# Bilinear hats of a deformable convolution: distances from ACT replaced by differences of clamped ramps

## The reference

```
def _bilinear_sample(x, py, px):
    y0 = jnp.floor(py); x0 = jnp.floor(px)
    for dy in (0.0, 1.0):
        for dx in (0.0, 1.0):
            yi = y0 + dy; xi = x0 + dx
            wy = 1.0 - jnp.abs(py - yi); wx = 1.0 - jnp.abs(px - xi)
            valid = (yi >= 0) & (yi < Hh) & (xi >= 0) & (xi < Ww)
            out = out + x[:, clip(yi), clip(xi)] * (wy * wx * valid)[None]
```

## Time and profile before

| | us |
|---|---|
| runs | 4312.64, 4316.48, 4319.70 |
| median | 4316.48 |
| span of the profiled execution | 4314.1 |
| PE, PEld busy | 3880.1 (90%), 2973.5 (69%) |
| DVE, ACT, POOL busy | 2952.5 (68%), 2786.4 (65%), 1140.5 (26%) |
| mean granted clock of PE | 0.94 of full speed |

### The profile page before, as it was taken

One profiled execution on the slowest core, in us unless ns is written; L12 is line 12 of the kernel. 1 busy time (PEld: TensorE's weight loads), 2 busy tenths in 40 slices (PEclk: granted clock), 3 DMA queues, 4 the chain that ended last, 5 costly groups with the idle time before them and its releaser, 6 DMA issues.

```text
span 4314.1 us, 221726 instructions
## 1 busy us (share of the span) xinstructions
PE 3880.1 (90%) x81908; PEld 2973.5 (69%) x81908; DVE 2952.5 (68%) x5858; ACT 2786.4 (65%) x6651; POOL 1140.5 (26%) x645
## 2 busy tenths in 40 slices
PE   4998799699789879979988997998799999799998
PEld 3776577477567657756765775776577777577776
DVE  5885687488567668847856884784577774577775
ACT  2885588388478658837865883885355554255554
POOL 0441243134033214403322431331111110111111
PEclk8999899799989989989998997999799999899999
DMA  4442544344244334424424443443766664666664
GB/s 125 127 127 66 143 125 110 89 126 127 75 132 126 90 106 127 125 76 131 126 71 127 127 114 92 126 125 109 179 154 152 150 150 127 147 154 152 152 150 110
DMA packets 244838, 533.50 MB, mean 124 GB/s; under 512 B 61200, under 2 KB 151824, under 8 KB 227216
## 3 DMA queue, kind: packets, MB, share of 16 engines
q1 hardware_dynamic: 194224, 498.67, 45.0%
q10 hardware_dynamic: 50240, 29.89, 2.4%
HBM read 471.87 MB, written 56.45 MB: 122 GB/s over the span
## 4 chain that ended last, share of the span: by engine, by line
PE 68%; SPq 18%; issue 7%; ACT 2%; DMA 2%; DVE 2%; POOLq 0%; ACTq 0%; DVEq 0%; POOL 0%; PEld 0%; PEldq 0%
PE P L544 26%; PE PS L562 24%; SPq L380 9%; PE P L515 8%; PE PS L575 8%; SPq L388 8%; SPq L370 1%; PE PS L515 1%; ACT H L848 1%; DMA X<-x_dram 1%; PE P L530 1%; DVE FOFF L1032 1%; DMA VT<-ht_store 0%; DVE A L917 0%; DVE ST L1036 0%
## 5 line engine op out<-in xcount | busy, mean ns | idle before, releaser
L917 DVE TENSOR_TENSOR A<-P,YC 121x384 f32<-121x384 f32 (+1 forms) x4608 | 2311.4, 550 | 850.1 <-ACT YC L768 684.5
L544 PE MATMUL P<-HL,SEL 32*121 32x384 f16 (+1 forms) x21504 | 1745.6, 304 | 131.6 <-issue 95.3
L768 ACT ACTIVATE YC<-P 121x384 f32<-121x384 f32 (+1 forms) x4608 | 1733.9, 444 | 98.7 <-PE P L544 65.8
L544 PEld LDWEIGHTS P<-HL,SEL 32*121 32x121 f16 (+1 forms) x21504 | 1126.9, 117 | 513.9 <-issue 228.6
L562 PE MATMUL PS<-A,VT 121*32 121x80 f32 (+1 forms) x40960 | 1342.7, 250 | 51.7 <-DMA VT<-ht_store 15.5
L562 PEld LDWEIGHTS PS<-A,VT 121*32 121x32 f32 (+1 forms) x40960 | 1093.0, 117 | 354.6 <-issue 200.4
L1103 POOL CAST HL<-DIST 128x1152 f16<-128x1152 f32 x320 | 366.3, 1145 | 3066.1 <-DVE DIST L922 3043.8
L745 ACT ACTIVATE SMP<-PS 128x480 f32<-128x480 f32 (+3 forms) x1152 | 593.9, 516 | 638.2 <-PE PS L562 632.9
L1105 POOL TENSOR_TENSOR HL<-DIST,HL 128x1152 f16<-128x1152 f32 x320 | 769.6, 2405 | 58.5 <-POOL HL L1103 58.5
L735 ACT ACTIVATE DIST<-HB,CONST 128x1152 f32<-128x1152 f32 x320 | 400.8, 1252 | 231.4 <-DMA HB<-off_store 128.8
L575 PE MATMUL PS<-SMP,CW 128*64 128x128 f32 x7424 | 476.0, 277 | 5.4 <-ACT SMP L745 5.4
(11 more groups left out here) (61 smaller groups left out, 703.4 us busy)
## 6 DMA issues: line engine op xcount, KB each, us to landing
HB<-off_store SPq DMA_DIRECT2D x2560, 72.0 KB
VT<-ht_store SPq DMA_DIRECT2D x256, 512.0 KB
VT<-ht_store SPq DMA_DIRECT2D x768, 132.0 KB
VT<-ht_store SPq DMA_DIRECT2D x256, 88.0 KB
off_store<-FOFF SPq DMA_DIRECT2D x160, 128.0 KB, 2.6
H<-x_dram SPq DMA_DIRECT2D x5, 2048.0 KB, 14.6
ht_store<-A ACTq DMA_DIRECT2D x32, 256.0 KB, 3.3
ht_store<-VT ACTq DMA_DIRECT2D x32, 256.0 KB, 3.9
```

Of the source, the lines that this page charges most:

```text
L544: mm = nc.tensor.matmul(dst, SEL[q, table, 0:sh.npos], hats, start=part == 0, stop=part == 1)
L768: nc.scalar.activation(YC[0:sh.npos, g % X_SLOTS, 0:sh.size], P[0:sh.npos, g % Y_SLOTS, 0:sh.size], ACT.Copy).then_inc(y_ready, 1)
L917: return nc.vector.tensor_tensor(dst, x, y, ALU.mult)
```

## The change

With r(q) = min(max(offset - (q - 1), 0), 1), a ramp that is clamped at both ends, the hat at position q is r(q) - r(q + 1). The change lets DVE compute max(HB + SCALE * (MARGIN + 1 - q), 0) straight from the offsets (`ramp`), POOL take the minimum with SCALE ahead of its two operations (into a new tile HAT), and SEL take the difference: 1 where q is the position, -1 where q is the position plus one. ACT's distance pass goes. The scale moves from SEL to ACT's copy of Y (1/SCALE squared). SP's wait is on the ramp instead of the distance. The two tables of SEL that are made per step need two DVE operations each instead of one. The tables of kind 1 come ready made from the host, like before, and the fallback gets three tables of its own.

```
-            def distance(band, half):
-
-                wait_alone(act, hb_full[half], 32 * IMG * (band + 1))
-                nc.scalar.activation(DIST[:, :], HB[:, half, :], ACT.Abs, bias=HAT_BIAS).then_inc(abs_done, 1)
...
-                            if sh.kind == 0 and g == sh.next_at and not last:
-                                next_distance(c + 1, band + half, 1 - half)
...
-                            if sh.kind > 0 and b == 0 and g == sh.next_at and not last:
-                                next_distance(c + 1, band + half, 1 - half)
...
-                distance(0, 0)
...
-                nc.vector.tensor_scalar(DIST[:, :], DIST[:, :], SCALE, SCALE, ALU.min, ALU.subtract).then_inc(clamp_done, 1)
+            def ramp(c, band, half):
+                if not isinstance(c, int):
+                    dve.wait_ge(hats_full, c)
+                wait_alone(dve, hb_full[half], 32 * IMG * (band + 1))
+                nc.vector.tensor_scalar(DIST[:, :], HB[:, half, :], RAMP_BIAS, 0.0, ALU.add, ALU.max).then_inc(ramp_done, 1)
...
                             if b == 0 and g == sh.next_at + 1 and not last:
-                                clamp(c + 1)
+                                ramp(c + 1, band + half, 1 - half)
...
-                nc.gpsimd.tensor_copy(HL[:, 0, half, :], DIST[:, :]).then_inc(hat_step, 1)
-                wait_alone(pool, hat_step, c + 1)
-                nc.gpsimd.tensor_tensor(HL[:, 1, half, :], DIST[:, :], HL[:, 0, half, :], ALU.subtract).then_inc(hats_full, 1)
+                nc.gpsimd.tensor_scalar(HAT[:, :], DIST[:, :], SCALE, None, ALU.min).then_inc(hat_step, 1)
+                wait_alone(pool, hat_step, 2 * c + 1)
+                nc.gpsimd.tensor_copy(HL[:, 0, half, :], HAT[:, :]).then_inc(hat_step, 1)
+                wait_alone(pool, hat_step, 2 * c + 2)
+                nc.gpsimd.tensor_tensor(HL[:, 1, half, :], HAT[:, :], HL[:, 0, half, :], ALU.subtract).then_inc(hats_full, 1)
...
-                                                 ACT.Copy).then_inc(y_ready, 1)
+                                                 ACT.Copy, scale=1.0 / SCALE ** 2).then_inc(y_ready, 1)
...
-                    sp.wait_ge(abs_done, c - 1)
+                    sp.wait_ge(ramp_done, c - 1)
...
-                    counted(nc.vector.tensor_scalar(SEL[:, axis, :], REL[:, axis, :], ST[:, 34 + axis:35 + axis], 1.0 / SCALE,
-                                                    ALU.is_equal, ALU.mult))
+                    counted(nc.vector.tensor_scalar(TMP[:, axis, :], REL[:, axis, :], 1.0, ST[:, 34 + axis:35 + axis],
+                                                    ALU.subtract, ALU.is_equal))
                 chained()
+                for axis in range(2):
+                    counted(nc.vector.scalar_tensor_tensor(SEL[:, axis, :], REL[:, axis, :], ST[:, 34 + axis:35 + axis], TMP[:, axis, :],
+                                                           ALU.is_equal, ALU.subtract))
...
-    consts[:, 5] = SCALE * (MARGIN - q)
+    consts[:, 5] = SCALE * (MARGIN + 1 - q)
```

More of the change, by code:

```diff
@@ L134, in build @@
         DIST = sb("DIST", [128, TAPS * CPX])
+        HAT = sb("HAT", [128, TAPS * CPX])
         HL = sb("HL", [128, 2, 2, TAPS * CPX], F16)
@@ L142, in build @@
         REL = sb("REL", [128, 2, 128])
-        SEL = sb("SEL", [128, 5, 128], F16)
+        SEL = sb("SEL", [128, 8, 128], F16)
         BIAS = sb("BIAS", [128, 3 * (LAYERS + 1)])
@@ L151, in build @@
         PS = ctx.enter_context(nc.psum_tensor("PS", [128, 512], F32))
-        HAT_BIAS = CONST[:, LAYERS + 1:LAYERS + 2]
+        RAMP_BIAS = CONST[:, LAYERS + 1:LAYERS + 2]
         AXIS_MASK = CONST[:, LAYERS + 2:LAYERS + 6]
@@ L185, in build @@
         hb_full = [sem(f"hb_full{i}") for i in range(2)]
-        abs_done = sem("abs_done")
-        clamp_done = sem("clamp_done")
+        ramp_done = sem("ramp_done")
         hat_step = sem("hat_step")
@@ L199, in build @@
         stepwise = [conv_full, conv_act, conv_dve, ht_full, ht_copied, ht_stored, off_full, off_ready, *off_stored, range_done,
-                    flag_step, *hb_full, abs_done, clamp_done, hat_step, hats_full, y_full, y_ready, x_full, product_done,
+                    flag_step, *hb_full, ramp_done, hat_step, hats_full, y_full, y_ready, x_full, product_done,
                     *vt_full, ps_full, ps_free, res_done, turn]
@@ L466, in step @@
                 load_offsets(0, 1)
-                sp.wait_ge(abs_done, 1)
+                sp.wait_ge(ramp_done, 1)
                 load_offsets(1, 0)
@@ L655, in fallback @@
                             pe.wait_ge(turn, base + T["spread", g])
-                            spread(sh, g, 0, 0, 4, 0)
-                            spread(sh, g, 0, 0, 2, 1)
-                            spread(sh, g, 0, 0, 3, 2).then_inc(turn, 1)
+                            spread(sh, g, 0, 0, 7, 0)
+                            spread(sh, g, 0, 0, 5, 1)
+                            spread(sh, g, 0, 0, 6, 2).then_inc(turn, 1)
                         for k in range(BLOCKS):
@@ L752, in read_sum @@
                     out_act(layer, PS[:, :], half, final).then_inc(ps_free, 1)
-                def next_distance(c, band, half):
-                    wait_alone(act, hats_full, c)
-                    distance(band, half)
                 def body(c, band, half, before, last):
@@ L917, in product @@
                 return nc.vector.tensor_tensor(dst, x, y, ALU.mult)
-            def clamp(c):
-                dve.wait_ge(abs_done, c + 1)
-                nc.vector.tensor_scalar(DIST[:, :], DIST[:, :], SCALE, SCALE, ALU.min, ALU.subtract).then_inc(clamp_done, 1)
+            def ramp(c, band, half):
[3 more added lines that the diff above has]
+                nc.vector.tensor_scalar(DIST[:, :], HB[:, half, :], RAMP_BIAS, 0.0, ALU.add, ALU.max).then_inc(ramp_done, 1)
             def body_of(sh, layer, group, final):
@@ L1058, in step @@
                 flag_count[0] += 1
-                clamp(0)
+                ramp(0, 0, 0)
                 chained()
@@ L1100, in hats @@
             def hats(c, half):
-                wait_alone(pool, clamp_done, c + 1)
-                nc.gpsimd.tensor_copy(HL[:, 0, half, :], DIST[:, :]).then_inc(hat_step, 1)
-                wait_alone(pool, hat_step, c + 1)
-                nc.gpsimd.tensor_tensor(HL[:, 1, half, :], DIST[:, :], HL[:, 0, half, :], ALU.subtract).then_inc(hats_full, 1)
+                wait_alone(pool, ramp_done, c + 1)
+                nc.gpsimd.tensor_scalar(HAT[:, :], DIST[:, :], SCALE, None, ALU.min).then_inc(hat_step, 1)
[3 more added lines that the diff above has]
+                nc.gpsimd.tensor_tensor(HL[:, 1, half, :], HAT[:, :], HL[:, 0, half, :], ALU.subtract).then_inc(hats_full, 1)
             def body_of(sh):
@@ L1128, in _tables @@
     rel = np.full((128, 2, 128), 99.0, np.float32)
-    sel = np.zeros((128, 5, 128), np.float32)
+    sel = np.zeros((128, 8, 128), np.float32)
     for axis in range(2):
@@ L1137, in _tables @@
         for n in range(16 * columns):
-            sel[:, 2 + tile, first + n] = is_x & (q == j + LANES * (n % columns))
-            sel[:, 4, first + n] = ~is_x & (q == n // columns)
+            for of, table, mine in ((j + LANES * (n % columns), tile, is_x), (n // columns, 2, ~is_x)):
+                sel[:, 2 + table, first + n] = 1.0 * (mine & (q == of)) - (mine & (q == of + 1))
+                sel[:, 5 + table, first + n] = (mine & (q == of)) / SCALE
     pxc = np.zeros((STRIPES, CH, STRIPE_ROWS, COLS), np.float32)
@@ L1155, in _tables @@
     far[:, CPX + CHUNKS:] = -np.where(is_x[:, None], 16 * (window % 4) + q[:, None], 16 * (window // 4) + q[:, None])
-    return dict(sel=(sel / SCALE).astype(np.float16).reshape(128, -1), rel=rel.reshape(128, -1),
+    return dict(sel=sel.astype(np.float16).reshape(128, -1), rel=rel.reshape(128, -1),
                 pxc=(SCALE * pxc).reshape(128, -1), consts=consts, far=SCALE * far)
```

## The result

The changed kernel takes 4787.74 us (median of four runs, 4774.16 to 4795.22) against 4314.56 us for the kernel before (four runs, 4312.64 to 4319.7). The ratio is 1.109, 95% interval 1.107 to 1.111: 10.9% slower. The forecast was 4302 us with a range of 4296 to 4345. Two of all the executions behind the numbers of this document were disturbed and are left out of the ratios, one of the kernel before (4729.95 us) and one of the kernel with half of the minimum (5701.88 us).

What follows compares the result with a forecast made beforehand. It took normal chunks to be bound by TensorE behind ACT and SP's issue time, 1% apart or less. 4314.1 - 15.4 + 0.4 = 4299.1, with 2.4 added back about 4302 us; range 4296 to 4345.

Steps and rivals of the forecast that it cites:

- The sizing of POOL's minimum: POOL's third operation, priced like the cast at 1.145 us plus 0.18 us wait, with the subtract's 2.405 us as upper bound.
- The point from which POOL sets the pace: In normal chunks, POOL's minimum may cost up to some 1.75 us before TensorE has to wait for POOL.
- The ring: Loop from a chunk's first Y spread through copy, products, ramp and POOL's three operations: 9.25 us with a 2.405 us minimum.
- rival 1: POOL's third operation makes its loop set the pace: +156 us, 4472 us, at a 2.405 us minimum; chance 0.19.
- SP's floor: SP's load issuing limits normal chunks to 8.55 or 8.67 us, with a last batch of 14.7 us per step.
- The gain of 15.4 us in the normal steps: TensorE's lag behind SP is taken back: 15.4 us in the four group 0 steps, 0 in the group 1 steps.
- TensorE's 0.66 us a chunk for the distance pass: From the sums to the first sampling part, ACT's distance pass costs TensorE 0.66 us: 2.71 against 2.05 us.
- TensorE alone at 8.33 us with the pass and 7.7 without: TensorE's own time per normal chunk, 8.33 us behind ACT's distance pass, falling to about 7.7 us once it goes.
- TensorE's waits for windows: Expected sign: in group 0 steps TensorE gains waits for window landings from about chunk 10 on.
- The final steps: The two final steps: no gain since ACT has slack, and 0.2 us each for the selection matrix, 0.4 us.
- Ramp: VectorE's ramp in the clamp's place takes 0.75 us, upper bound 1.25, and can start up to 1.25 us earlier.
- Scale on ACT's copies: A constant factor on the 12 Y copies per chunk: taken as 0, at most 0.6 us a chunk.

Runs made afterwards that it cites:

- the kernel with half of the minimum: The changed kernel with the minimum split by columns, POOL taking 576 of 1152 and VectorE the rest: 4544.63 us, ratio 1.052.
- the kernel with busy matmuls: The changed kernel with six unread matmuls before TensorE's wait for the hats in each normal chunk: 4718.92 us, ratio 1.0936.
- the four kernels that had cheap hats: From the changed kernel: minimum on VectorE, 4361.7 us; copy on POOL, 4312.67; VectorE's minimum in normal steps only, 4317.58; that with old distances in final steps, 4299.96.
- the kernel without the pass: The changed kernel with the minimum on VectorE in normal steps and the earlier kernel's distance scheme in final steps: 4299.96 us, ratio 0.9968.

## Why the prediction was wrong

*The sizing of POOL's minimum* is the step that failed. The price was taken from the cast, 1.145 us, since "one input is what it has", with the subtract, 2.405 us, as the upper bound. It takes 3.13 us, outside both. A bound by the nearest rows is none if neither row is of the operation: no tensor_scalar of POOL was in the trace. The copy in its place, 1.15 us, takes the loss away: 4312.67 us. It doesn't bring the 4302 us forecast, since the final steps take back most of the gain.

*The point from which POOL sets the pace* was the second error: 1.75 us, by the two rings read here 1.12 to 1.25. The ring was written down in rival 1 (2.0 + 0.75 + 0.17 + 1.145 + 2.42 + 0.36 = 6.85 us without the minimum), 0.58 us short of 7.43. Missing were 0.29 us from POOL's end to TensorE's start, 0.24 us in the head (0.11 with the copy, at full clock; the rest goes with the low clock), and 0.06 in the ramp. At 1.75 the ring would pass 8.6 us by the sum on record; by the measured one the forecast's own 1.145 us already stood on the edge, 0.1 us from it: that it would have cost nothing was luck.

*Rival 1, POOL sets the pace, is what happened*, at a chance of 0.19, and its mechanism is right. Its size was far off, +156 us with 4472 in all as the worst case. Put the measured price into its formula: 6.85 + 3.13 = 9.98 us, +1.38 x 240 = 331 us. Measured were 464 in the normal steps. The ring's missing 0.58 us a chunk are the difference; about 69 us of it go with TensorE's clock, as the kernel with busy matmuls shows.

*SP's floor* held: pairs of 17.09 and 17.34 to 17.39 us and last batches of 14.4 to 15.5 us, once 16.35, in every kernel whose ring was shorter and whose loads were issued as before. *The gain of 15.4 us in the normal steps* was right in size: 15.0, 12.7, 11.8 and 16.6 us in the four kernels that had cheap hats, each from one trace, and 13.2 between the medians for the last of them, whose final steps are as before. Where it lay was not: with the copy the four group 0 steps gave 8.7 us and not all, the four group 1 steps 4.0 and not 0. The last batches of group 0 did fall, by 2.8 to 4.3 us, 14.2 together, but a part of that was lost again elsewhere in the same steps; where, was not traced.

*TensorE's 0.66 us a chunk for the distance pass* is in the rows, for from the sums to the first sampling part it is 2.06 us with the copy, as forecast, but the chunk gets only 0.24 us shorter; where the other 0.4 us go was not traced. So *TensorE alone at 8.33 us with the pass and 7.7 without* were both too low: 8.59 and 8.35. That the two bounds stood 1% apart is right by the 8.59, not by the 8.33 that the prediction had. TensorE's waits for windows came as said, 15 of them between 140 and 340 us in the kernel without the pass.

*The final steps*, 0.4 us forecast, were 13.1 us. The kernel with the copy lost 5.3 there and the one with POOL's minimum in these steps alone 12.8, so 7.5 us go with the minimum's price even in a chunk of 17.7 us. How much of the 5.3 is the third operation, the ramp or the tables wasn't taken apart.

*Ramp*: 0.81 us against 0.75, its bound 1.25. *Scale on ACT's copies*: 0.496 us a copy against 0.500, nothing, as said. *SP's wait for the ramp, the larger SEL*: nothing was seen of them in the normal steps. *The residual*: its mean in the normal form rose from 0.56 to 0.98 us, not the 0.3 us counted; hidden in the ring, and so still worth nothing here. *ACT's busy time* fell by 274 us and not 400. The durations of its instructions, added up one by one, did fall by 411; but busy time counts a stretch in which two of them overlap once, and with more idle time between them fewer overlap.

## What to carry to other kernels

An operation that moves to another engine has no price until a row of that engine, that operation and that shape gives one. If there is none, the range must hold a case well above the nearest rows (the minimum was 2.7 times the one and 1.3 times the other), and it should be looked up what the ring then does.

Before a third operation is put in series, add up the whole ring from a row to its own repetition, wake-ups between engines included, and compare that sum with the pace of the loop. Here the two were within 0.1 us even with the cheapest operation tried, at an engine that was 26% busy before; starting the ramp earlier in the ring, with POOL's work as it was, gave back 293 of 464 us.

Where two bounds lie 1% apart, lifting one shows almost nothing. Before the change is called worthless, read the pace in a stretch where the other bound doesn't hold yet, or lift the other too, but not onto the engine under test: the same edit gave 17 us as it stood and 177 with loads moved to ACT, where the early chunks of a step say some 55.

## What the runs showed of the hardware

- POOL, 128 partitions, float32: cast to float16 or copy of 1152 columns 1.15 us, two-input add 2.66, two-input subtract to float16 2.39, minimum with a constant 3.13; of 576 columns 1.81.
- VectorE's minimum with one constant took 0.76 us for the same 1152 columns, a quarter of POOL's time.
- VectorE's residual (two SBUF inputs) that starts inside an operation of POOL ends with it: 1.91 us for 0.34, and in the kernel with busy matmuls a mean of 1.70 us for 264 of them.
- TensorE starts 0.28 to 0.33 us after the POOL operation that it waits for, POOL 0.17 to 0.20 after VectorE's and 0.17 to 0.19 after its own.
- TensorE idle 0.8 us once a chunk: granted clock 0.86 in that stretch, 20 matmuls 2.40 us instead of 1.31. With six more matmuls in the gap 0.98, and 69 us less.
- A load of 144 KB whose source has a dimension of 2 outermost landed after 20 us, one of 72 KB with 16 outermost after 2.4; SP's issue took 0.61 us and more instead of 0.31.
